# A relational graph convolution whose first head is moved in among its product tiles: maxima, weights and sums of head 0 between the products of one layer

## What is computed

```python
xr = jnp.einsum('nd,rdf->rnf', x, W)
oi = xr[etype, dst]
oj = xr[etype, src]
qi = oi @ q
kj = oj @ k
alpha = jax.nn.leaky_relu(qi + kj, NEG_SLOPE)
m = jax.ops.segment_max(alpha, dst, num_segments=n_nodes)
e = jnp.exp(alpha - m[dst])
z = jax.ops.segment_sum(e, dst, num_segments=n_nodes)
a = e / (z[dst] + EPS)
msg = (a[:, :, None] * oj.reshape(-1, heads, out_ch)).reshape(-1, heads * out_ch)
out = jax.ops.segment_sum(msg, dst, num_segments=n_nodes)
```

## Time and profile before

| quantity | value |
|---|---|
| median of 3 runs | 1673.07 us (1672.65 to 1674.59) |
| profiled execution, its own time | 1675.66 us |
| its span in the trace | 1673.7 us |
| mean granted clock of TensorE | 0.991 of full speed |
| PE busy, share of the span | 1617.6 us, 97% |
| DVE / ACT / POOL busy | 1079.7 / 684.5 / 651.7 us |

### The profile page before, as it was taken

How to read it: one execution, slowest core, us unless ns; L and a number is a source line. 1 busy time by engine, 2 the same in 40 slices (tenths; PEclk the granted TensorE clock), 3 DMA queues, 4 the chain that set the end, 5 groups by cost and what they waited for, 6 DMA issues and landing times. The chain is left out here.

```text
span 1673.7 us, 23124 instructions
## 1 busy us (share of the span) xinstructions
PE 1617.6 (97%) x8371; PEld 1417.9 (85%) x8371; DVE 1079.7 (65%) x2095; ACT 684.5 (41%) x1095; POOL 651.7 (39%) x606
## 2 busy tenths in 40 slices
PE   7899999999999999999988999899999999999998
PEld 4378899999999998789867989888888888999977
DVE  8757888787787877875888567763323322444646
ACT  4334534434444344434766553333343234232231
POOL 0042252333423414237877755214443334433421
PEclk9999999999999999999999999999999999999999
DMA  4256031222322223123000323113222223323241
GB/s 127 76 192 215 29 122 57 86 80 64 122 66 67 90 99 114 48 104 123 29 0 20 107 73 105 63 42 110 75 88 91 82 70 94 98 70 107 85 138 43
DMA packets 57178, 145.34 MB, mean 87 GB/s; under 512 B 13936, under 2 KB 17136, under 8 KB 56048
## 3 DMA queue, kind: packets, MB, share of 16 engines
q1 hardware_dynamic: 50448, 111.11, 21.5%
q10 hardware_dynamic: 6624, 32.77, 5.5%
HBM read 131.80 MB, written 12.06 MB: 86 GB/s over the span
## 5 line engine op out<-in xcount | busy, mean ns | idle before, releaser
L913 POOL TENSOR_TENSOR w_pair<-early,w_pair 128x384 fp32r<-128x384 f32 x468 | 490.4, 1086 | 865.6 <-ACT w_pair L1685 865.3
L997 PE MATMUL ps<-w_pair,cols_x 128*128 128x384 f32 x2088 | 375.7, 336 | 1.8 <-POOL w_pair L913 1.2
L997 PEld LDWEIGHTS ps<-w_pair,cols_x 128*128 128x128 f32 x2088 | 363.2, 188 | 5.0 <-DVE cols_x L2115 1.8
L1685 ACT ACTIVATE w_pair<-early 128x768 fp32r<-128x768 f32 x234 | 182.2, 838 | 299.6 <-PE ps L997 130.0
L997 PE MATMUL ps<-w_pair,wide 128*128 128x384 f32 x1728 | 302.4, 334 | 0.3 <-DVE early L2118 0.3
L997 PEld LDWEIGHTS ps<-w_pair,wide 128*128 128x128 f32 x1728 | 300.1, 188 | 1.5 <-DVE early L2118 0.6
L1622 PE MATMUL ps<-wide,w_pair 128*128 128x512 f32 x972 | 227.7, 392 | 3.4 <-DVE wide L2115 3.4
L1622 PEld LDWEIGHTS ps<-wide,w_pair 128*128 128x128 f32 x972 | 181.0, 188 | 44.0 <-DVE wide L2115 5.8
L1570 PE MATMUL ps<-prob,wide 128*128 128x512 f32 x546 | 136.8, 390 | 0.0
L1135 PE MATMUL ps<-prob,wide 128*128 128x512 f32 x576 | 135.8, 395 | 0.2 <-DVE yt L2217 0.2
L1135 PEld LDWEIGHTS ps<-prob,wide 128*128 128x128 f32 x576 | 108.0, 188 | 26.4 <-issue 3.8
(11 more groups left out here) (333 smaller groups left out, 2173.6 us busy)
## 6 DMA issues: line engine op xcount, KB each, us to landing
early<-weights SPq DMA_DIRECT2D x246, 384.0 KB, 3.1
edge_mask<-counts ACTq DMA_DIRECT2D x13, 512.0 KB, 3.3
multi<-attn ACTq DMA_DIRECT2D x8, 768.0 KB, 4.3
kept<-early ACTq DMA_DIRECT2D x3, 1536.0 KB, 5.9
counts<-tally SPq DMA_DIRECT2D x12, 256.0 KB, 4.5
multi<-kept ACTq DMA_DIRECT2D x2, 1536.0 KB, 6.6
edge_mask<-masks ACTq DMA_DIRECT2D x5, 512.0 KB, 3.3
last_raw<-weights SPq DMA_DIRECT2D x6, 384.0 KB, 5.3
```

The lines of the kernel that those rows point to most:

```text
L913: return nc.gpsimd.tensor_tensor(dst, whole, high.bitcast(F32), ALU.subtract)
L997: mm = nc.tensor.matmul(ps[:, m, 0:HW], left[:, a, k, m * P:(m + 1) * P], w_pair[:, slot_of[0], b, k, :], start=(k == 0 and a + b == 0), s ...
L1685: return nc.scalar.activation(dst, src, ACT.Copy)
```

## The change

The change moves head 0 in among the product tiles.

- The maxima are taken in another order: the three relations of head 0 first. `relation_uv` then runs twice, for head 0 alone behind the third maxima, and for heads 1 to 3 behind the last. The third relation's mask gets a place of its own and is loaded earlier, and the counts are loaded at tile 2 instead of tile 7.
- TensorE transposes u and v of head 0 behind tile 6 (`turn_first_uv`), spreads them behind tiles 7, 8 and 9, runs the weighted tiles 0 to 7 behind tiles 10 to 17 and 8 to 11 behind tiles 20 to 23. The transposition for the other heads stands behind tile 19. Maxima 5 to 11 share bank 5 and are spread behind tiles 5 and 11 to 16.
- Because banks 0 and 1 now take head 0's sums, product tiles from 8 on alternate between banks 2 and 3, so each waits for the copy of the tile two before it.
- ACT runs the steps of items 0 to 14 behind tiles 8 to 23. On DVE, maxima 5 to 11 stand behind items 3 to 9, and the second `relation_uv` stands before the start of item 10.
- The split of pass 38 (the next layer's first weights), which stood behind tile 19, goes in thirds behind the first three pieces of result in heads 1 and 2, on ACT and on POOL.

```diff
+LATE = 8
+FIRST_SUM = 10
+RELATION_ORDER = [(r, 0) for r in range(REL3)] + [(r, h) for h in range(1, HEADS1) for r in range(REL3)]
+SPREAD_BANK = (7, 4, 6, 7, 4, 5, 5, 5, 5, 5, 5, 5)
+SPREAD_AT = {2: 2, 3: 3, 4: 4, 5: 5, 11: 6, 12: 7, 13: 8, 14: 9, 15: 10, 16: 11}
+SUM_AT = {t: t - FIRST_SUM if t < 18 else t - 12 for t in (10, 11, 12, 13, 14, 15, 16, 17, 20, 21, 22, 23)}
+STEPS_AT = {8: (0, 2), 9: (2, 3), 10: (3, 5), 11: (5, 6), 12: (6, 7), 13: (7, 8), 14: (8, 9), 15: (9, 10), 16: (10, 11), 17: (11, 12),
+            21: (12, 13), 22: (13, 14), 23: (14, 15)}
+LOWS_BEFORE = {12: (4, 5), 13: (5, 6), 14: (6, 7), 15: (7, 8), 16: (8, 9), 17: (9, 10), 18: (10, 11), 22: (11, 12), 23: (12, 13)}
+def late_bank(t):
+    return 2 + t % 2 if t >= LATE else t % NB
...
+            def part_low(slot, count, p):
+                pool.wait_ge(w_high, count + (p + 1))
+                whole = w_raw[:, p]
+                low_of(w_pair[:, slot, 1, 2 * p, :], whole[:, 0], w_pair[:, slot, 0, 2 * p, :])
+                low_of(w_pair[:, slot, 1, 2 * p + 1, :], whole[:, 1], w_pair[:, slot, 0, 2 * p + 1, :]).then_inc(w_low, 1)
...
+                        if 8 * r + u in before:
+                            item_lows(*before[8 * r + u])
...
-                        if m == 3 and first_pass + 2 * r + n not in (39, 44, 45):
+                        if m == 3 and first_pass + 2 * r + n not in (38, 39, 44, 45):
...
+                        if 2 * h + c < 3:
+                            pool.wait_ge(x_lo, W_AT + i + 1)
+                            part_low(0, 3 * 38, 2 * h + c)
+            relation_low(64, 34, before=LOWS_BEFORE)
+            item_lows(LOWS_BEFORE[23][1], len(items))
...
-                r, h = i // HEADS1, i % HEADS1
+                r, h = RELATION_ORDER[i]
                 if i >= 2:
+                    pe.wait_ge(max_done, 9 + max([k + 1 for k in range(i) if SPREAD_BANK[k] == SPREAD_BANK[i]] + [2 if i == 5 else 0]))
...
+            def turn_first_uv():
+                pe.wait_ge(uv0_ready, 1)
+                for m in range(NB):
+                    mm = nc.tensor.transpose(ps[0:48, 6, m * P:(m + 1) * P], uvc[:, 48 * m:48 * (m + 1)], ident[:])
+                mm.then_inc(uv0_turned, 1)
...
-            for r in range(REL3):
-                for u in range(8):
-                    n, m = u // 4, u % 4
-                    slot_of[0] = n
-                    if r == 0 and n == 0:
-                        product(32, m, cols_x, row_read, 4 + m + 1, turned=KB)
-                    else:
-                        product(32 + 2 * r + n, m, cols_x, tile_copied, 64 + 8 * r + 4 * n - 4 + m + 1)
-                    t = 8 * r + u
...
-                    elif t < REL3 * HEADS1:
-                        spread_relation(t)
-                    elif t == 16:
-                        turn_all_uv()
-                    elif t == 17:
-                        pe.wait_ge(q_ready, 30)
-                        spread_v(0)
-                    elif t == 18:
-                        spread_u(0)
-                        spread_v(1)
-                    elif t == 19:
-                        spread_u(1)
-            pe.wait_ge(tile_copied, 86)
...
+            for t in range(REL3 * 8):
+                relation_tile(t)
+                if t == 0:
+                    attention_rows()
+                elif t == 1:
+                    pe.wait_ge(alpha_lo, 1)
+                    spread_relation(0)
+                    attention_columns()
+                    spread_relation(1)
+                elif t == 6:
+                    turn_first_uv()
+                elif t == 7:
+                    pe.wait_ge(uv0_copied, 1)
+                    spread_v(0)
+                elif t == 8:
+                    spread_u(0)
+                    pe.wait_ge(max_done, 13)
+                    spread_v(1)
+                elif t == 9:
+                    spread_u(1)
+                elif t == 19:
+                    turn_all_uv()
+                if t in SPREAD_AT:
+                    spread_relation(SPREAD_AT[t])
+                if t in SUM_AT:
+                    weighted_tile(SUM_AT[t])
+                if t == 20:
+                    pe.wait_ge(q_ready, 30)
+                    spread_v(3)
+                elif t == 21:
+                    spread_u(3)
+            for tile in range(NB * REL3, NB * rounds):
+                weighted_tile(tile)
...
+            def item_steps(first, end):
+                for i in range(first, end):
+                    result_tile = i < len(items) - 1 and items[i][2] is not None
+                    for stage in (high_item, exp_item) if result_tile else (exp_item, high_item):
+                        stage(i)
-                    if t == 7:
-                        act.wait_ge(max_done, 13)
-                        act.dma_start(mask[:], masks[3]).then_inc(mask_in, 16)
+                    if t == 2:
+                        act.wait_ge(max_done, 10)
                         for i in range(REL3):
                             act.dma_start(count16[i], counts[SLOT3 + i]).then_inc(cnt_in, 16)
-                    copy_tile(32 + 2 * r + n, m, n, 64 + t, rows[r], lows=t, dots_done=64)
-                    if m == 3 and t < 23:
+                    copy_tile(32 + 2 * r + n, m, n, 64 + t, rows[r], lows=t, dots_done=64, bank=late_bank(t))
+                    if m == 3 and t < 19:
                         split_high(34 + 2 * r + n, n)
+                    elif t == 5:
+                        nc.scalar.activation(zc[:, 1, 0:1], mx[:, 0:1], ACT.Exp, scale=0.0)
                     if t == 0:
                         act.wait_ge(alpha_done, 1)
                         copy(alpha[0:48, :], ps[0:48, 6, :]).then_inc(alpha_hi, 1)
-                    if t == 16:
+                    elif t == 6:
+                        act.wait_ge(uv0_turned, 1)
+                        copy(alpha0[0:48, :], ps[0:48, 6, :]).then_inc(uv0_copied, 1)
+                    elif t == 7:
+                        copy_v1(0)
+                    elif t == 8:
+                        copy_v1(1)
+                    elif t == 11:
+                        copy_v1(2)
+                    elif t == 19:
                         act.wait_ge(misc_done, 69)
                         nc.scalar.activation(alpha[64:112, :], alpha[64:112, :].bitcast(F32), ACT.Copy, scale=0.0)
-                        copy(alpha[0:48, :], ps[0:48, 6, :]).then_inc(q_ready, 12)
-                    elif t == 17 or t == 18:
-                        copy_v1(t - 17)
-                    elif t >= 19:
-                        exp_item(t - 19)
-                        high_item(t - 19)
-            for i in range(5, len(items) + 1):
-                result_tile = i < len(items) - 1 and items[i][2] is not None
-                for stage in (high_item, exp_item) if result_tile else (exp_item, high_item):
-                    stage(i)
+                        copy(alpha[0:48, :], ps[0:48, 5, :]).then_inc(q_ready, 12)
+                    elif t == 20:
+                        copy_v1(3)
+                    if t in STEPS_AT:
+                        item_steps(*STEPS_AT[t])
+            item_steps(STEPS_AT[23][1], len(items) + 1)
...
-            for i in range(REL3 * HEADS1):
-                r, h = i // HEADS1, i % HEADS1
-                if r == 1:
+            def relation_maxima(i):
+                r, h = RELATION_ORDER[i]
+                if r == 0:
+                    dve.wait_ge(mask_in, 32)
+                elif r == 1:
                     dve.wait_ge(mask2_in, 16)
                 else:
-                    dve.wait_ge(mask_in, 32 + 8 * r)
-                maxima(i + 1, mx1[:, r, h], 10 + i, 84, bank=(7, 4)[i % 2], spread=spread_done, mask=mask2 if r == 1 else mask)
-                if i == 0:
-                    dve.wait_ge(alpha_cols, 1)
...
-            relation_uv(HEADS1)
+                    dve.wait_ge(mask3_in, 32)
+                maxima(i + 1, mx1[:, r, h], 10 + i, 84, bank=SPREAD_BANK[i], spread=spread_done, mask=relation_masks[r],
+                       halves=[late_scratch[:, :, m * D + HW:m * D + HW + 256] for m in range(NB)] if i > 4 else None)
+            mark(nc.vector.memset(uvc[:], 0.0))
+            mark(nc.vector.memset(alpha0[:].bitcast(F32), 0.0))
+            relation_maxima(0)
+            dve.wait_ge(alpha_cols, 1)
...
+            relation_maxima(1)
+            relation_maxima(2)
+            relation_uv(slice(0, 1), uv0_ready)
+            dve.wait_ge(uv0_ready, 1)
+            relation_maxima(3)
+            relation_maxima(4)
...
+                if 3 <= i < 10:
+                    relation_maxima(i + 2)
+                if i == 9:
+                    relation_uv(slice(1, HEADS1), uv_ready)
```

More of the change, by code:

```diff
@@ L680, in graph_layers @@
         v_bc = sb("v_bc", [P, N], F32)
+        with nc.sbuf_tensor("alpha0", [P, N], F32R) as alpha0:
+            pass
         r_den = sb("r_den", [P, N], F32)
@@ L984, in _, with product @@
         def _(pe):
```

(32 more changed lines are left out.)

148 lines of the change are left out of this document (76 added, 72 removed).

## The result

The changed kernel takes 1686.59 us in the median of 4 runs (1682.89 to 1687.66), the kernel before 1673.83 us in 4 runs beside it (1672.65 to 1674.92). The ratio is 1.0073, with a 95% interval of 1.006 to 1.0085: slower by 12.8 us, or 0.7%. The profiled execution took 1687.66 us.

What follows compares the result with a forecast made beforehand. The prediction took TensorE, busy for 97% of the span, to bound the kernel. Its terms, 0.35 + 4.5 + 0.6 + 2.4 + 2.2 + 1.0 = 11.05 us, added to 1673.07 gave 1684 us, range 1675 to 1691.

Steps and rivals of the forecast that it cites:

- The base of the argument: Product stage and head 0: TensorE has no idle time up to about 839 us, so moving head 0 fills none.
- Turning twice: Transposing u and v a second time on TensorE: four more transpositions, +0.35 us.
- The wait behind tile 6: Before the first transposition: POOL stretches `relation_uv`, TensorE idles 2.8 us, slow clock costs 1.7; +4.5 us.
- The spread of u behind tile 8: TensorE waits for ACT's copy of v for head 0, queued behind tile 7's copies and split; +0.6 us.
- The wait before tile 19: ACT's late copies of tile 17, behind the second `relation_uv`: 1.6 us idle and half a clock loss; +2.4 us.
- The lead at head 1: DVE starts item 17 2.05 us behind weighted tile 12 instead of 0.15 ahead; the lag reaches TensorE, +2.2 us.
- the faster rival: A longer lead of the items at head 1 removes the wait at 843 and its slow clock: 1669 us, chance 0.06.
- Pass 38's split in the heads: Heads 1 and 2: POOL's moved steps slow DVE's weigh; a third of the bound 2.9 taken, +1.0 us.
- DVE is the pace there: Head 1: DVE sets the pace; a head costs TensorE 23.5 us of work and took 27.8.
- The signs named in advance: New profile: 2 to 3 us idle near 750 with lower clock, waits before tile 19 and in head 1, late item 17.
- neither wait appears: Rival: small steps nearly free or POOL elsewhere, so no waits behind tile 6 or before tile 19; 1676 to 1677, chance 0.22.
- the second wait in full: Rival: POOL also stretches the second `relation_uv`, before tile 19; 5.0 us more, 1689 us, chance 0.15.

Runs made afterwards that it cites:

- e2: The kernel before with only the split of pass 38 moved in thirds behind the first three pieces of result in the heads: 1679.07 us, ratio 1.0027.
- e3: The changed kernel with items 14 and 15 ahead of tile 23's copies on ACT, and POOL's low steps of items 13 and 14 earlier: 1683.38 us, ratio 1.0051.
- e5: The changed kernel with the edits of e1 and e3 together: 1677.87 us, ratio 1.0022.
- e1: The changed kernel with the split of pass 38 put back behind product tile 19: 1680.83 us, ratio 1.0036.
- e6: The changed kernel with the split of pass 34, and POOL's six low steps of it, behind tile 5 instead of tile 3: 1685.23 us, ratio 1.0068.
- e4: The changed kernel with head 0's first transposition, the spreads and the first items one tile later: 1687.73 us, ratio 1.0073.
- e11: e8 with ACT's copy of v for head 0 ahead of the split at tile 7: 1677.35 us, ratio 1.0021.
- e12: e5 with only the second `relation_uv` moved behind the start of item 10: 1678.5 us, ratio 1.0017.
- e8: e5 with the edit of e6, and the second `relation_uv` behind the start of item 10: 1680.13 us, ratio 1.0035.

## Why the forecast was right, and which terms were not

The forecast of 1684 us, slower by 11.05, met 1686.59 and 12.8, in the range and on the right side. No version came below before. The base of the argument held: up to about 839 us TensorE had no idle time to give, and the product stage got longer by 3.84 us. But the sum was nearer than its terms: two errors of 4 to 5 us cancelled, and that is luck. By the table the change costs 10.5 us up to tile 47; the rest of the 12.8 lies outside the stretch that was rearranged.

- **Turning twice**, forecast 0.35: the transpositions take 752.57 - 752.19 = 0.38.
- **The wait behind tile 6**, forecast 4.5 (2.8 idle and 1.7 of slow clock): measured 1.3 and no slow clock. Place, releaser and cause were right. The size was wrong in two ways. I had counted 9 small steps before POOL's rows end and 12 got through, so that `relation_uv` took 9.86 us; that is the bound of 1.2 us that the forecast had from the old 9.8 us and passed over. The subtraction that was to hold one more step (752.06) came when all were done but the last. And I had taken the fall of the clock behind one wait of 2.35 us as the rule for a wait of this size; in e2 the same wait of 2.35 us before the same spread is followed by no fall.
- **The spread of u behind tile 8**, forecast 0.6: measured 0.3.
- **The wait before tile 19**, forecast 2.4: measured 0.9 and no slow clock. The steps were close: from the end of tile 16 (798.26) the maxima end at +3.1, `relation_uv` at +8.4 (forecast 8.8), the exponential starts at +9.2, the copies end at +11.3 (forecast 11.8). TensorE is there at +10.4 (forecast 10.2). A difference of two such times carries the errors of both.
- **The rest of the product stage**: 3.84 - 0.38 - 1.28 - 0.3 - 0.9 leaves 1.0 us that no term had. It lies in the product tiles themselves. From the start of one to the next instruction (or to the wait) the 23 of them sum to 72.97 us in the timeline, before to 71.94; 0.17 of that is counted in the 1.28. A tile between spreads takes 3.12. One ahead of a weighted tile mostly takes 3.15 (763.51 to 766.66), one that ends in a wait about 3.3 (tiles 6, 8 and 18), and the ones beside a transposition 3.20 to 3.24.
- **The lead at head 1**, forecast 2.2: the column 12 to 18 has +2.45. The start of item 17 lies 2.61 us behind weighted tile 12 (836.72 and 834.11; forecast 2.05), and e3 gives back 3.6 by that alone. It gives more than was lost: in e3 DVE starts item 17 0.91 us ahead of tile 12, before 0.15. So "no order gives more" lead, the ground on which the faster rival was held down, was wrong: e3 and e5 do the first half of head 1 in 13.7 us where before takes 14.84. It was not enough to reach the other side.
- **Pass 38's split in the heads**, forecast 1.0 and at most 2.9: measured 4.9 (e2) to 5.8 (e1) in the medians, 4.7 and 4.5 in the column 18 to 24. This is the step that failed. I looked at POOL's share of busy time (20.69 of 27.80) and at how a POOL step slows one on DVE. What decides is POOL's order: 2.75 us of subtractions (from 859.94) stand ahead of a low step that takes 1.25 us and whose result TensorE is ready to use at 862.17 (863.97 - 1.80), and DVE's `weigh` needs the slot that the low step still reads. Behind that comes a weighted tile at half clock, 1.6 us more. The trace of before had the sign of it: beside the 5.0 us for ACT that the prediction read, TensorE waited 4.5 us for POOL's low steps in the heads, so "DVE is the pace there" left out the second engine that sets it.

The waits of the product stage (forecast 7.5, measured 2.5) were 5.0 too high, the split about 4 too low. The signs named in advance were met in part: near 750 TensorE idled 1.1 us and not 2 to 3, and no lower clock followed. Of the rivals, "neither wait appears" did not come; nor did the second wait in full.

The Trainium skill ("VectorE: DVE Perf Modes", the section on the TRN2 errata) had given 1.6 us for the 23 steps as an estimate, from 58 + N cycles each. Without most of POOL's work (e6) they take 4.5, and a free step of 4 elements takes 0.15 to 0.17 us, so the measurement decides against that figure. The same section of the skill says itself that this figure is too low and that the fixed part was measured as about 150 cycles; by that, an estimate, such a step takes 0.16 us, and the traces agree. The rule of the Trainium skill's "SBUF — State Buffer", the section on who interferes with whom, that only the port pair shared by VectorE and GpSimd causes contention, agrees with one step that takes 0.16 us free (e6) and 0.93 beside POOL's subtractions (after).

What stays open: why removing each wait of the product stage (e4, e6, e11) gives it back within four tiles. Each of these traces names another releaser, and I did not find an order that has none. Only the wait before tile 19 went for good in that stage (e12), and the best product stage (102.93) is still 2.9 us longer than before. Open too is what lowers the granted clock behind one wait and not behind another of the same length.

## What to carry to other kernels

Work moved into a stretch where an engine is free on average can still be late for what is queued behind it: look for the next instruction on that engine that another waits for, and count the moved work in full if it is due sooner than the moved work lasts. Where TensorE has no idle time, interleaving two stages adds waits there, even if the engines beside it have room; what it can gain lies further on, here at most 1.7 us in the heads against 2.9 to 3.8 lost in the product stage. A forecast that sums several short waits, each the difference of two long chains, may be right in the sum alone; check the terms before trusting its reasons.

## What the runs showed of the hardware

The fall of the granted clock is not told by the length of the wait before it. Behind 2.78 us (851.07) it stayed at 1.00, behind 1.80 us (863.97, with a wait of 1.17 just before) it was 0.53; in e8 a wait of 2.03 was followed by a tile of 4.87 us, in e11 one of 1.99 by one of 3.31. Nor is it told by the place. The wait of 2.35 us before weighted tile 18 is followed by 0.56 in the kernel before and by 1.00 in e2; the wait of 2.78 us at that place by 1.00 in the changed kernel and by 0.50 in e6. First the row of e2, then that of e6:

```profile
844.20:847.60 3.40, 2.97 (x12) 2.15 (x13) 1.71 (x3) 1.69 (x3) 3.40 (x3) 1.00 0.31 98
```
```profile
852.70:856.10 3.40, 3.40 (x8) 2.72 (x9) 1.71 (x3) 1.66 (x3) 3.40 (x3) 0.50 0.36 110
```

The last pair has the same waits ahead of it (1.11 and 0.55 us, and 1.07 and 0.55) and the same busy times of the other engines behind it (DVE 1.70 and 1.71, POOL 3.40 both), so neither row tells the fall in advance. A fall costs about 1.6 us where it comes (weighted tile 22 takes 3.42 instead of 1.84), nearly as much as the wait itself.

POOL's subtraction of 384 elements takes 0.98 us beside DVE's small steps (5.88 for 6) and 1.37 in the heads (2.75 for 2), where DVE runs 512-element steps with two inputs. Two steps that come due together show both outcomes: DVE 0.68 us and POOL 1.83 (e5), or DVE 1.80 and POOL 1.27 (e12, both at 873.5). The same two rows stand 0.02 us apart in e8 (as in e5) and in e11 (as in e12) too, so either outcome occurs at the same distance, and it is worth 1.1 us to the work behind it.
